# Ten buffers of expert rows in place of six, and the zeros kept in the buffers of the results

## What is computed

```python
x = x + tanh(g_xattn) * attention(layernorm(x), ctx, ctx, ...)   # 16 heads, 120 keys
z = layernorm(x)
scores = z @ gate_w + gate_b                        # 8 experts
topk_vals, topk_idx = top_k(scores, 2)
p = softmax(topk_vals)
h = relu(einsum('td,edf->etf', z, w1) + b1)         # 128 -> 512, for each expert
y = einsum('etf,efd->etd', h, w2) + b2              # 512 -> 128
x = x + tanh(g_ffn) * (sum over the two chosen experts of p * y)
```

## Time and profile before

| what | us |
|---|---|
| median of three timed executions | 430.51 |
| lowest, highest of the three | 429.17, 568.55 |
| the profiled execution, its own time | 428.97 |
| its span, first to last instruction | 427.2 |

### The profile page before, as it was taken

How to read it: one execution, slowest core, us unless ns; L and a number is a source line. 1 busy time by engine, 2 the same in 40 slices (tenths; PEclk the granted TensorE clock), 3 DMA queues, 4 the chain that set the end, 5 groups by cost and what they waited for, 6 DMA issues and landing times.

```text
span 427.2 us, 12274 instructions
## 1 busy us (share of the span) xinstructions
PE 383.2 (90%) x4245; PEld 310.6 (73%) x4245; DVE 293.0 (69%) x1075; ACT 267.9 (63%) x828; POOL 256.8 (60%) x280
## 2 busy tenths in 40 slices
PE   2889999999999999999999999988999999999500
PEld 1457776777777777778777768887999999999500
DVE  4887887888788887888898985755643333333176
ACT  2467868878787887878788783333444544444254
POOL 5363536457779688698794554454666667665500
PEclk9999999999999999999999998999999999999855
DMA  3999999952000000000000196556868799895198
GB/s 83 233 282 411 413 411 390 239 97 58 28 21 15 23 21 14 28 17 20 28 9 21 36 267 195 170 174 172 240 194 285 233 275 286 272 301 175 37 310 281
DMA packets 47195, 72.20 MB, mean 169 GB/s; under 512 B 7974, under 2 KB 31662, under 8 KB 47134
## 3 DMA queue, kind: packets, MB, share of 16 engines
q1 hardware_dynamic: 42813, 62.44, 48.2%
q0 software_dynamic: 4320, 8.99, 6.0%
HBM read 41.94 MB, written 34.20 MB: 178 GB/s over the span
## 4 chain that ended last, share of the span: by engine, by line
PE 76%; DVE 10%; ACT 6%; DMA 3%; issue 3%; SPq 1%; POOL 1%; POOLq 0%; DVEq 0%; ACTq 0%
PE S L790 14%; PE T L772 7%; PE S L670 7%; PE U L772 7%; PE S L681 6%; PE O L702 6%; PE O L710 5%; PE T L689 5%; PE U L689 5%; ACT P L862 5%; DMA yg<-res 2%; PE S L796 2%; PE E L662 2%; DVE nmax L1158 1%; PE E L651 1%
## 5 line engine op out<-in xcount | busy, mean ns | idle before, releaser
L862 ACT ACTIVATE P<-S,nmax 128x120 f32<-128x120 f32 x512 | 137.1, 411 | 40.5 <-DVE nmax L1158 40.5
L1016 POOL DMA_INDIRECT zs<-z,posu x64 | 64.6, 1010 | 53.8 <-PE O L710 25.5
L1027 POOL DMA_INDIRECT res<-yo,dpos x71 | 68.0, 957 | 36.9 <-PE S L796 21.2
L1158 DVE TENSOR_REDUCE nmax<-S 128x4 f32<-128x480 f32 x128 | 75.1, 649 | 18.8 <-PE S L681 14.3
L790 PEld LDWEIGHTS S<-wbuf,H 128*128 128x128 f32 x568 | 73.5, 192 | 3.3 <-issue 0.2
L790 PE MATMUL S<-wbuf,H 128*128 128x128 f32 x568 | 74.6, 275 | 0.0
L670 PE MATMUL S<-mb_r,I_r 128*128 128x480 f32 x128 | 63.2, 496 | 4.6 <-ACT P L862 3.2
L906 ACT ACTIVATE H<-T,wbuf 128x256 f32<-128x256 f32 (+1 forms) x82 | 31.7, 445 | 41.6 <-PE T L772 41.6
L906 ACT ACTIVATE H<-U,wbuf 128x256 f32<-128x256 f32 (+1 forms) x78 | 30.5, 449 | 37.4 <-PE U L772 37.3
L977 POOL TENSOR_SCALAR z<-X,mv,rstd 128x128 f32<-128x128 f32 x56 | 44.2, 794 | 10.6 <-PE O L710 7.1
L989 POOL TENSOR_SCALAR Kb<-Kt,hm 128x480 f32<-128x480 f32 x28 | 41.4, 1486 | 13.0 <-PE O L745 6.3
(11 more groups left out here) (174 smaller groups left out, 628.2 us busy)
## 6 DMA issues: line engine op xcount, KB each, us to landing
wbuf<-wpk SPq DMA_DIRECT2D x40, 578.0 KB, 5.0
zs<-zero SPq DMA_DIRECT2D x1, 17952.0 KB, 60.5
yg<-res SPq DMA_DIRECT2D x16, 256.0 KB, 4.2
zin<-zs SPq DMA_DIRECT2D x31, 132.0 KB, 4.6
wpk<-in_w SPq DMA_DIRECT2D x1, 2048.0 KB, 57.6
wpk<-in_w SPq DMA_DIRECT2D x8, 256.0 KB, 8.8
out<-X SPq DMA_DIRECT2D x16, 128.0 KB, 3.6
ctx_sb<-in_ctx SPq DMA_DIRECT2D x1, 1440.0 KB, 16.7
```

The costliest lines, as they stand in the source:

```text
L862: ins = nc.scalar.activation(P[:, n % 4, j, :], a[:, j * LK:(j + 1) * LK], ACT.Exp, bias=nmax[:, n % 4, j:j + 1])
L1016: nc.gpsimd.indirect_dma_start(out=zs, out_offset=bass.IndirectOffsetOnAxis(ap=posu[:, F, k, i:i + 1], axis=0), in_=z2[:, F % 2, i, :], in ...
L1027: nc.gpsimd.indirect_dma_start(out=res, out_offset=bass.IndirectOffsetOnAxis(ap=dpos[:, n % NDP, h:h + 1], axis=0), in_=yo[:, n % NYO, h, ...
L1158: v.tensor_reduce(nmax[:, n % 4, :], Sb[n % NHG][:, 0:HG * LK].rearrange("p (j k) -> p j k", j=HG), AX_X, ALU.max, negate=True).then_inc(m ...
```

## The change

`zin` has ten buffers in place of six. The tile `zero` of its own is gone; the zeros are written to the first 1056 numbers of each partition of `yo`, which is first written with results in step 2 of the expert work, and the clearing DMA reads them there. `zero` had 4224 bytes in each partition, and the four more buffers of `zin` have the same 4224 bytes (4 x 2 x 132 numbers of 4 bytes).

```diff
-NZ = 6
+NZ = 10
...
-        zero = sb("zero", [128, ZROW])
...
         yg = sb("yg", [128, NYG, UB, 2, D])
+        zero = yo[:].rearrange("p n h d -> p (n h d)")[:, 0:ZROW]
...
             sp.wait_ge(prep_pool, 4)
             sp.dma_start(zs.rearrange("(p n r) d -> p n (r d)", p=128, r=ZROW // ZW),
-                         zero[:].unsqueeze(1).broadcast_to((128, ROWS // 128 * ZW // ZROW, ZROW))).then_inc(zs_clear, 16)
+                         zero.unsqueeze(1).broadcast_to((128, ROWS // 128 * ZW // ZROW, ZROW))).then_inc(zs_clear, 16)
...
-            nc.gpsimd.memset(zero[:], 0.0).then_inc(prep_pool, 1)
+            nc.gpsimd.memset(zero, 0.0).then_inc(prep_pool, 1)
```

## The result

The changed kernel took 437.84 us (median of four; 436.74 to 440.27), the kernel before 430.27 (median of four). The ratio is 1.0176 with an interval of 1.0139 to 1.0213: slower, by 1.4 to 2.1%, some 7.6 us. The profiled execution took 437.32 us with a span of 435.5. The forecast was 436.4 us, 7.4 us above the profiled execution of the kernel before.

The account below looks back on a forecast made before the run. The prediction took TensorE, busy for 383.2 of 427.2 us, to bound the kernel. The profiled 428.97 us plus 5.7 us of wait and 1.7 of clock gave 436.4 us, with a range of 433.0 to 440.2.

Parts of the forecast that it names:

- Nothing to win: In the expert work TensorE has no wait for `zin` or `wbuf`, so four more row buffers have no wait to remove.
- Zeros in `yo`, 0: At the clearing: same memset and DMA with another address, before `yo` gets its first result; cost 0.
- Opening and phase 1, 0: Four more row loads at the opening, and rows 12 before weights 8: SyncE has time to spare; cost 0.
- Rows 16 ahead of weights 13: In SyncE's order at phase 2, weights 13 stand behind the wait for all scatter groups and leave 14.5 us late.
- The wait, 5.7 us: At half 26 TensorE stands from 314.93 us until weights 13 land at 320.67: 5.7 us, 4.9 to 6.9.
- Weights 14 to 16, 0: Behind the wait these loads are late too, but only weights 14 can miss TensorE's need; taken as 0.
- The reserve of up to 0.9 us: Kept for the range: weights 14 could arrive up to 0.9 us late for TensorE after the wait.
- Rival A: After the wait, weights 14 to 16 pile up on the DMA engines, 1 us more each: 439.4 us; chance 0.15.
- The clock, 1.7 us: After the stall TensorE's clock falls to half speed for 3.4 us, losing 1.7 us; bounds 0 and 3.4.
- rival C: TensorE's clock does not fall at the wait; the stall alone gives 434.7 us; chance 0.10.
- Rivals B and D: B: early rows relieve the crowded loads, 429.0 us, chance 0.05. D: SyncE's scatter wait is empty, 429.0 us, chance 0.03.
- The sum: For the whole kernel: 5.7 us of wait plus 1.7 of clock, 7.4 us, nothing to win back.

Follow-up runs that it names:

- run 2: The changed kernel with ten buffers, but SyncE issues rows of tile 16 and after only once weights of tile 15 are out; 1.0002 of the kernel before.
- the first run: The kernel before with its six buffers of rows, only the zeros moved into the results' buffers `yo`; 0.9992 of the kernel before.

## Why the prediction was right, point by point

- **Nothing to win.** TensorE waited for no rows before, so more room for rows could remove no wait. With ten buffers and the old order (run 2) the time is that of before.
- **Zeros in `yo`, 0.** Shown by the first run: 0.9992 (0.9959 to 1.0024).
- **Opening and phase 1, 0.** Weights 6, 7 and 8 left at 268.54, 272.49 and 277.82 us, 0.25 us behind those of the earlier trace rows, as all of that stretch is; TensorE shows no wait there.
- **Rows 16 ahead of weights 13.** Forecast: rows at 314.95 and weights at 316.17 us; seen: 315.09 and 316.25.
- **The wait, 5.7 us.** It was 5.3. Weights 13 took 4.2 us to land where I took 4.5, which is 0.3 us less; half 26 was due 0.25 us later and the load left 0.1 us later. The estimate by the Trainium skill ("DMA: Bandwidth & Descriptors") was 3.4 us, and the trace disagrees with it by 0.8 us. The section "Anatomy of one DMA" gives its 2.0 us for DMAs that GpSimd issues; this load is issued by SyncE, so the estimate was stretched beyond what the page states.
- **Weights 14 to 16, 0.** No wait for them in the changed kernel. The reserve of up to 0.9 us shows only where the clock doesn't fall: 0.4 us in the run with early scatters. Rival A, a pile of late weights, did not come. (Its 8.6 us is too little: four weight loads and five of rows are 2972 KB of 1024 bytes, which take 9.1 us at 335 GB/s; that is still under 11.)
- **The clock, 1.7 us.** The mechanism was right and the term too small: 2.4 us, so rival C, no fall, did not come. I took the 3.4 us of the stretch at 256 us as time at half speed behind the wait. It held from 320.49 to some 325.2 us, 4.7 us, half of which is 2.4. The fall itself, at about 318.4 us, lay in the idle time and cost nothing. The Trainium skill ("TensorE: Matmul & The Clock Gate", HAM oscillation) says that a wait for a DMA lets the array start slow; the pair of runs with and without products agrees, 6.26 against 3.83 us. My ground for expecting the fall was weaker than it looked, though. I set a pause of 1.9 us that left the clock at 1.00 against one of 5.7, but in other runs that same pause was followed by a fall (last section), and the fall at 256.7 us, from which I took the price, had no pause ahead of it longer than 0.8 us. The pause of 1.9 us could not carry the argument; that the long wait would end at half clock came true.
- **Rivals B and D.** Rows early did not help, as the run with rows 16 held back shows too, and the wait for the scatters was not empty: 15.8 us.
- **The sum.** 7.4 forecast, 7.7 us seen between the due time of half 26 and half 28, two errors against each other (-0.4 and +0.7). The rest of the 8.3 us of span, 0.25 ahead of it and 0.35 us in the tail, belongs to no step of mine and was not looked into; two executions of the kernel before, 429.17 and 430.51 us, differ by more. That 436.4 is 1.4 us under the measured median comes mostly from the base: I added to the profiled 428.97 us and not to the median. Between the medians the change cost 7.6 us.

No version here beats the kernel before; those with rows 16 held back, with seven buffers and with the zeros alone equal it.

## What to carry to other kernels

More buffers let a queue run further ahead, and where one instruction stream issues two kinds of load, running ahead in one kind moves its waits in front of the other kind. Before deepening a prefetch, write out the order in which the queue will issue and look for a load that waits for something produced late (a table, a scatter); whatever stands behind it is late too. Where that can't be helped, hold the deeper stream back at the phase boundary, and count for a stall of some us on TensorE also the steps that then run at half clock: 1.7 to 2.6 us here, behind each of the seven waits of 3.4 us and more.

## What was not expected of the hardware

- **What a fall of the clock costs depends on how long the low level lasts behind the wait.** Behind a wait of 5.1 to 5.3 us two steps lost 2.4 to 2.5 us in each of three profiles of this order (the changed kernel twice, nine buffers: 323.73 to 329.91 us in its TensorE timeline, 6.2 in place of 3.7), and 2.6 behind the 4.7 us of the run with weights first. After a wait of 6.9 us, with ten buffers and own zeros, they lost 1.9 (326.44 to 332.10), after those of 3.4 and 3.7 us, with eight buffers, 1.7.
- **The length of a wait does not tell whether the clock falls.** All seven waits for weights of 3.4 us and more were followed by a fall or had one in them. But the wait of 1.9 us for VectorE's rows left the clock at 1.00 in six of the fourteen profiles, both of the kernels compared here among them, and in the eight others it fell within 1.4 us of the end of that wait (2.4 us long in one of them). So it did in the run of the zeros alone: its clock was 0.60 within 284 to 285 us and then 0.50 until within 287 to 288. TensorE's timeline of that run, and the row of the clock on its page, where the second of the two eights is this fall:

```profile
284.11 1.01 PE L730 MATMUL E<-I,z 128*128 128x128 f32 x4 [1.91 <-DVE z L1403]
...
PEclk9999999999999999999999989899999999999955
```

  What decides between the two was not tested. The waits for weights of 1.2 and 1.8 us left the clock at 1.00, once each, which with this says little. An execution can be longer by such falls with nothing changed in the kernel: in the second set, executions of the kernel before whose mean clock was 0.967 to 0.970 took 429.0 to 430.7 us, those with 0.960 or 0.961 took 431.6 to 434.3.
- **Two chips differ more than the change.** The same kernel before took 430.3 us in the second set, and 441.9 and 444.6 in the two others, which ran on one chip. In the profiles of these two sets, engines stop for up to some 1 us with nothing to wait for that the profile shows, as in TensorE's waits of the repeated run of the changed kernel:

```profile
PE T L772 <- issue: 3.9, 7, 0.9
```

  In the first profile of the changed kernel this row is not there. What stops them is open. With it rows 16 left 2.3 to 4.0 us behind the last scatter's end in these two sets, and 2.2 in the second set, which is one reason why only ratios within a set are compared.
- **A 128x512 product in float32 took 0.86 us**, twice 0.43, so a filler has to be measured before it is counted.
